# Attention one: where the two transpositions of the normalised input stand in an even pass

## The reference

```python
h = W.T[tokens]                                  # 8 x 1024 x 256
x = (h - mean(h)) / sqrt(var(h) + 1e-5)
xh = x.reshape(b, c, 16, 16).transpose(0, 2, 1, 3)   # 16 heads of width 16
q, k, v = split(xh @ Wqkv + bqkv)
att = softmax((q @ k.T) / 4 * tril(ones, k=-1))  # masked scores are 0, not -inf
h = h + (att @ v) @ Wr + br
```

## Time and profile before

| | |
|---|---|
| time, median of 3 runs | 2886.16 us (2885.0 to 2889.22) |
| time of the profiled execution | 2895.28 us |
| its span, first to last instruction | 2893.5 us |
| mean granted TensorE clock | 0.947 |
| PE busy (share of the span) | 2526.1 us (87%) |
| DVE busy | 2120.3 us (73%) |
| ACT busy | 1510.1 us (52%) |
| POOL busy | 1639.9 us (57%) |

### The profile page before, as it was taken

One profiled execution on the slowest core, in us unless ns is written; L12 is line 12 of the kernel. 1 busy time (PEld: TensorE's weight loads), 2 busy tenths in 40 slices (PEclk: granted clock), 3 DMA queues, 4 the chain that ended last, 5 costly groups with the idle time before them and its releaser, 6 DMA issues. The chain is left out here.

```text
span 2893.5 us, 58186 instructions
## 1 busy us (share of the span) xinstructions
PE 2526.1 (87%) x15254; PEld 1485.1 (51%) x15318; DVE 2120.3 (73%) x5672; ACT 1510.1 (52%) x3246; POOL 1639.9 (57%) x2560
## 2 busy tenths in 40 slices
PE   3888888888888888888868999999999889999999
PEld 1333334433334433333355666666666656666666
DVE  6667767667677667776467999999999866555564
ACT  1555556555556555556504655555555544444444
POOL 6753333443333443343246878777877667677775
PEclk7899999999999999999869999999999989999999
DMA  4533433433433433443140000000000000000000
GB/s 109 111 72 59 68 59 57 66 58 58 67 60 57 66 58 59 66 67 56 26 142 1 1 1 0 0 0 0 0 0 0 1 6 17 15 16 15 15 16 19
DMA packets 81254, 112.93 MB, mean 39 GB/s; under 512 B 25100, under 2 KB 37144, under 8 KB 80536
## 3 DMA queue, kind: packets, MB, share of 16 engines
q1 hardware_dynamic: 76360, 101.44, 20.5%
q0 software_dynamic: 3072, 8.39, 1.0%
q10 hardware_dynamic: 1744, 2.16, 0.2%
HBM read 18.98 MB, written 8.39 MB: 9 GB/s over the span
## 5 line engine op out<-in xcount | busy, mean ns | idle before, releaser
L693 DVE TENSOR_REDUCE cand<-ring 128x4 f32<-128x512 f32 x1152 | 714.0, 681 | 348.4 <-PE ring L806 326.1
L596 ACT ACTIVATE probs<-scoresT 128x512 f32<-128x512 f32 x1152 | 624.5, 605 | 588.0 <-PE scoresT L746 537.5
L746 PE MATMUL scoresT<-stage 98*128 98x512 bf16 (+3 forms) x1536 | 381.7, 340 | 43.0 <-ACT probs L596 28.8
L513 POOL TENSOR_SCALAR_AFFINE_SELECT probs<-probs 128x256 f32<-128x256 f32 x512 | 203.8, 413 | 319.4 <-ACT probs L596 312.4
L766 PE MATMUL pv<-probs,Vg 128*32 128x512 f32 (+3 forms) x3072 | 330.9, 553 | 17.9 <-POOL probs L513 15.9
L806 PE MATMUL ring<-Km,Qm 64*128 64x512 bf16 (+2 forms) x1792 | 228.6, 321 | 77.7 <-DVE cand L693 40.8
L1238 PE MATMUL mm<-w_W,hT 128*128 128x256 f32 x1024 | 243.6, 381 | 8.4 <-ACT z L1326 3.5
L1258 PE MATMUL mm<-w_W,x2T 128*128 128x512 f32 x512 | 242.2, 595 | 0.3 <-DVE x L1477 0.2
L746 PEld LDWEIGHTS scoresT<-stage 98*128 98x128 bf16 x1536 | 121.9, 99 | 220.7 <-ACT probs L596 130.4
L1319 ACT ACTIVATE hT<-mmT,w_be,w_g 128x128 f32<-128x128 f32 x512 | 185.5, 469 | 76.8 <-PE mmT L1249 76.8
L806 PEld LDWEIGHTS ring<-Km,Qm 64*128 64x128 bf16 x1792 | 76.3, 95 | 269.8 <-issue 130.8
(11 more groups left out here) (255 smaller groups left out, 5269.4 us busy)
## 6 DMA issues: line engine op xcount, KB each, us to landing
stage<-parts SPq DMA_DIRECT2D x256, 96.0 KB
Qm<-parts SPq DMA_DIRECT2D x128, 128.0 KB
Km<-parts SPq DMA_DIRECT2D x128, 128.0 KB
stage<-parts SPq DMA_DIRECT2D x256, 64.0 KB
stage<-parts SPq DMA_DIRECT2D x256, 32.0 KB
out<-result SPq DMA_DIRECT2D x64, 128.0 KB, 1.7
stage<-ct SPq DMA_DIRECT2D x128, 4.0 KB
w_W<-in_W SPq DMA_DIRECT2D x4, 512.0 KB
```

Of the source, the lines that this page charges most:

```text
L513: nc.gpsimd.affine_select(out=d, in_=d, compare_op=ALU.is_gt, fill=0.0, base=0, pattern=[[0, 2], [1, P]], channel_multiplier=-1).then_inc( ...
L596: nc.scalar.activation(probs[:, buffer(slot), :], scoresT[slot % SCORE_BANKS][:], ACT.Exp, scale=SOFT).then_inc(exp_ok, 1)
L693: ins = nc.vector.tensor_reduce(c, src[:].rearrange("p (t a b) -> p t a b", t=c.shape[1], b=P), AX.X, ALU.max)
L746: ins = nc.tensor.matmul(scoresT[slot % SCORE_BANKS][:, at:at + hi - lo], Ks[0:ROWS, gi, hh, P * kt:P * kt + P], Qs[0:ROWS, gi, hh, lo:hi] ...
```

## The change

In the table of an even pass the two parts of `XT` move from behind slots 4 and 7 to behind slots 5 and 8, that is, behind the 5th and 8th bank, counted from 0.

```diff
 AT = {
-    0: {"LN_NORM": (1, 2, 4, 5), "XT": (4, 7), "PV_COPY": 4, "EQ": 6, "TMP": 0, "PT": 5, ... "PV_HALF": 17},
+    0: {"LN_NORM": (1, 2, 4, 5), "XT": (5, 8), "PV_COPY": 4, "EQ": 6, "TMP": 0, "PT": 5, ... "PV_HALF": 17},
     1: {"LN_STATS": (9, 13, 20, 24), "PV_COPY": 4, "EQ": 6, "TMP": 0, "PT": 5, "WR": 2, "V": 8, "VG": 6, "LOAD": 0, "PV_HALF": 17},
```

More of the change, by code:

```diff
@@ L145 @@
 AT = {
-    0: {"LN_NORM": (1, 2, 4, 5), "XT": (4, 7), "PV_COPY": 4, "EQ": 6, "TMP": 0, "PT": 5, "OT": 24, "WR": 25, "RSUM": 3, "SUF": 12, "QK": (9, 13, 17, 20), "MID_LAG": 2, "V": 21, "VG": 5, "LOAD": 0, "PV_HALF": 17},
+    0: {"LN_NORM": (1, 2, 4, 5), "XT": (5, 8), "PV_COPY": 4, "EQ": 6, "TMP": 0, "PT": 5, "OT": 24, "WR": 25, "RSUM": 3, "SUF": 12, "QK": (9, 13, 17, 20), "MID_LAG": 2, "V": 21, "VG": 5, "LOAD": 0, "PV_HALF": 17},
     1: {"LN_STATS": (9, 13, 20, 24), "PV_COPY": 4, "EQ": 6, "TMP": 0, "PT": 5, "WR": 2, "V": 8, "VG": 6, "LOAD": 0, "PV_HALF": 17},
```

## The result

The changed kernel takes 2911.44 us (2909.56 to 2913.81) against 2887.69 us for the kernel before (2885.0 to 2890.38): a ratio of 1.0088, with a 95% interval from 1.0075 to 1.0100, or 23.75 us more. Forecast were 21.8 us more.

The account below looks back on a forecast made before the run. PE leads at 87% busy; within the even pass DVE bounds up to k5, PE behind it. Terms 0 + 0 + 9.8 (shift) + 12.0 (clock falls) = 21.8 us on the 2886.16 median give 2908.0 us; range 2890 to 2916.

Parts of the forecast that it names:

- S5 ahead of XT0: In PE's stall ahead of XT0: S5's 0.22 us falls into the 1.52 us wait; value nothing.
- XT1's leaving its place: Ahead of PT1: PE gets early, k5 stays put, its wait grows from 0.21 to some 1.7 us; value nothing.
- The rival in which PT1 times the meeting: At k5: PT1, not DVE, times the second `acc`; 0.65 us gained per pass, 9.1 us faster, 2877; chance 0.06.
- XT1 behind k5: Behind k5 and S8: 0.53 us of transpositions plus 0.17 us bank wait, QK 0.70 us later; 9.8 us over 14 passes.
- Not hidden later: From QK on: nothing taken off the 0.70 us per pass; the rival, hidden in a later wait, about 2887, chance 0.12.
- The falls: Behind k5: the thin stretch ahead drops TensorE's clock to half in 8 of 14 passes, 1.5 us each, 12.0 us.
- The chance of one half for this case: Whole kernel: shift and clock falls together, 21.8 us slower, 2908.0 us, chance 0.50; shift alone, 2896.0, had 0.30.

Follow-up runs that it names:

- VG late on the kernel before: Kernel before, with DVE's VG moved behind slot 8 in both kinds of pass: 2874.97 us, 10.2 us less than before, ratio 0.9970.
- filler at k5: Changed kernel plus four extra 512-column products per even pass in PE's wait ahead of k5: 2908.94 us, 11.8 us over the kernel before.
- changed, again: The changed kernel unaltered, run once more beside the kernel before on another chip: 2909.52 us, 24.3 us over before, ratio 1.0087.
- filler at CT: Kernel before plus three extra 512-column products ahead of each small transposition CT: 2920.78 us, 23.6 us over before, ratio 1.0081.
- the change with VG late: Changed kernel with DVE's VG moved behind slot 8 in both kinds of pass: 2906.79 us, 20.8 us over the kernel before, ratio 1.0072.

## Why the prediction was right

- *S5 ahead of XT0: nothing.* Right: XT0 alone moved gives +1.8 us with an interval around none. A term of 0.08 us per pass was missed, in DVE's `xn`, which makes 1.1 us over 14 passes.
- *XT1's leaving its place: nothing, with k5 at the same place.* Right but for these 0.08 us. The wait ahead of k5 was put at 1.7 us and is 1.73. The rival in which PT1 times the meeting falls: PT1 now starts 248.26 - 246.73 = 1.53 us behind XT0, where it was 349.84 - 346.92 = 2.92, and the addition comes no sooner behind k2's reductions. (The rival's 1.35 us was misread: by the earlier trace rows S7 ends at 348.11 + 0.60 = 348.71, which leaves 1.13. Nothing hangs on it.) It was half true all the same, as VG late on the kernel before shows: PT1 was level with VG.
- *XT1 behind k5: 0.70 us.* It is 0.75: 0.50 us of transpositions (252.02 to 252.52) against 0.53, and the gap from S8 to XT1 leaves 252.02 - 251.55 - 0.23 = 0.24 us for the bank wait against 0.17. The changed kernel's profile doesn't name DVE for this gap; that of XT1 right behind k5 does.
- *Not hidden later.* Right for the way to k6, which is 0.75 us longer too, and in the total as far as the filler at k5 can tell: without the falls behind k5 the loss is 11.8 us, but not below 8.
- *The falls: 8 of 14, 1.5 us each, 12.0 us.* The mechanism is right, its count too low. There are 12 of them, and each adds 6.04 - 4.71 = 1.33 us to the way from k5 to k6, up to 1.6 where it starts later.

The means over the 13 halves, in us, show where the loss lies:

| kernel | XT0 to k5 | k5 to k6 | k6 to the next XT0 | a half |
|---|---|---|---|---|
| before | 4.16 | 3.96 | 78.35 | 86.48 |
| changed | 4.20 | 6.09 | 78.09 | 88.38 |
| changed, again | 4.19 | 6.22 | 78.42 | 88.84 |
| changed, filler at k5 | 4.24 | 4.71 | 78.87 | 87.82 |

From k5 to k6 the changed kernel loses 2.13 us per half: 0.75 are the shift, 9.8 us over the 13 halves, and 1.38 the clock, 17.9 us where the sum had 12.0 for 14. From k6 on the half is 0.26 us shorter, which gives 3.4 us back, and which nothing in the forecast foresaw. (The second profile has 1.51 us for the clock and gives nothing back; the only profile of the kernel before, which I set both against, starts up as those of the slower chip do.) So the terms were right in kind, the term of the falls was some 6 us too low, and that 21.8 came so near to the measured 23.75 is in part luck. The last row says the same from the other side: the filler takes 1.4 us per half off the way from k5 to k6, and only 0.6 to 1.0 us of it reach the whole half. The places of the other falls move too.

The chance of one half for this case stands beside two rules of the Trainium skill (TensorE: Matmul & The Clock Gate). The one that ties the fall to a long single gap (HAM oscillation — how this bites in real kernels) would have given 9.8 us. It does not hold here, as the clock falls behind a wait of 1.73 us that follows a stretch with work in it. The one on frequent short idles as PSUM banks are cycled (A second HAM failure mode: psum-queue depth-cycling, of the same page of the Trainium skill) agrees with the trace in that the clock falls without a long gap. The filler at k5 shows that filling one such wait keeps the clock up behind it; that it takes frequent ones no run here shows.

What stays open is what slows the four `xn` by 0.08 us, and what places the falls when a half is 88.75 us long. Three quite different kernels settle at 88.7 to 88.8 us (the filler at CT, the change with VG late, and XT1 behind S9, whose halves alternate between 88.1 and 89.4), with falls at regular places. The sum of single terms holds in such a kernel only as long as the falls don't move.

## What to carry to other kernels

Find the instruction at which two engines meet, and ask of each move whether it crosses it: here 0.5 us of PE's work was free at both places tried ahead of k5, and behind it cost 0.75 us where S8 stood ahead of it and 1.0 us (1.87 - 0.88) where nothing did. Where a wait is put down to an engine, look at what that engine does just ahead of the releasing instruction; moving VG, 0.43 us that nobody waited for, out of DVE's way gave 10 us, and 17 with PT1 out of the tie. Before filling a wait, look at what ends it: the filler at CT cost 0.67 us wherever CT waited for its bank. And count what a longer wait does to TensorE's clock: half of this loss or more was dense work at 1.2 GHz behind a thin stretch.

## What the runs showed of the hardware

- Four extra products per pass, 1.0 us of TensorE work in a wait, kept the granted clock behind them at 1.0 in all 14 passes; without them it was at 0.5 in 13 and 14 of 14. The loss against the kernel before was 11.8 us with them and 24.3 without, on two chips.
- The clock also fell behind 2.15 us of work in 3.00 (filler at CT, 388.4 us), where ahead of the other falls shown PE had 1.17 and 1.27 us of work in 3.00.
- The gain of an edit can vanish in the clock's falls: 0.34 us saved in each pass moved the changed kernel from 24.3 to 20.8 us over before, on two chips and with intervals that overlap, while the same edit on a kernel without falls behind k5 moved it from -0.7 to -17.0 on one.
- One and the same kernel is 12 us apart between chips (2897.2 and 2885.2 us). Whatever the kernel, the profiles of the slower one begin the first even pass 8 us later, so that absolute expectations were off where differences were not.
